# Attention with a low-rank conditioner: x loads and splits placed anew, the projection table shifted by one part

## What is computed

```python
c = x @ W.T + b + 2 * (x @ A[i]) @ B[i]      # A[i], B[i]: rank 16, one pair for each batch
q, k, v = c @ w_q, c @ w_k, c @ w_v           # 32 query heads, 8 key and value heads of 32
x = x + softmax(q k^T / sqrt(32)) v @ w_o
y = x @ weight[j].T                           # one of 8 matrices for each batch
x = x + 4 * sum_e gate_e(y) * (y @ A_e.T) @ B_e.T   # top 2 of 4 experts, rank 16
```

## Time and profile before

| | us |
|---|---|
| median of 3 runs | 1071.86 (1070.69 to 1072.41) |
| the profiled execution | 1075.97 |
| its span | 1074.3 |

### The profile page before, as it was taken

How to read it: one execution, slowest core, us unless ns; L and a number is a source line. 1 busy time by engine, 2 the same in 40 slices (tenths; PEclk the granted TensorE clock), 3 DMA queues, 4 the chain that set the end, 5 groups by cost and what they waited for, 6 DMA issues and landing times.

```text
span 1074.3 us, 17421 instructions
## 1 busy us (share of the span) xinstructions
PE 1018.2 (95%) x6934; PEld 822.1 (77%) x6934; DVE 635.1 (59%) x1071; ACT 450.3 (42%) x782; POOL 233.7 (22%) x224
## 2 busy tenths in 40 slices
PE   7999999999899998999989999899799999999997
PEld 6878787877578775777767787577488898898896
DVE  6562734567755578654776557664555655655653
ACT  5121223355544466543664556544523323323320
POOL 1000001133223333223331236443200100100100
PEclk9999999999899998999998999899989999999998
DMA  7030312011421124211132125435757667667531
GB/s 257 0 99 18 111 55 72 22 36 37 116 57 37 35 53 115 58 34 31 45 97 71 44 81 153 115 115 175 225 165 233 210 189 230 213 184 231 196 118 40
DMA packets 49888, 117.41 MB, mean 109 GB/s; under 512 B 7298, under 2 KB 26114, under 8 KB 45712
## 3 DMA queue, kind: packets, MB, share of 16 engines
q1 hardware_dynamic: 40080, 81.70, 26.0%
q0 software_dynamic: 9728, 34.61, 10.1%
HBM read 86.38 MB, written 18.89 MB: 98 GB/s over the span
## 4 chain that ended last, share of the span: by engine, by line
PE 83%; DVE 6%; ACT 4%; DMA 4%; POOL 1%; SPq 1%; issue 1%; ACTq 0%
PE psP L752 17%; PE psW L1038 16%; PE psF L254 11%; PE psG L1066 8%; PE psO L820 5%; PE psT L807 4%; PE psS L796 4%; PE psP L767 3%; PE psX L1281 3%; PE psO L824 3%; DVE q_stack L652 2%; PE psY L1300 2%; ACT probs L599 2%; ACT q_stack L565 1%; PE psF L265 1%; PE psM L831 1%
## 5 line engine op out<-in xcount | busy, mean ns | idle before, releaser
L672 DVE TENSOR_REDUCE nmax<-psS 128x2 f32<-128x512 f32 x256 | 164.7, 685 | 178.5 <-PE psS L796 176.8
L549 POOL TENSOR_TENSOR p_sum<-probs 128x512 f32<-128x512 f32 x128 | 167.1, 1305 | 395.3 <-ACT probs L599 395.1
L752 PE MATMUL psP<-x_hl,wq 128*128 128x512 f32 x960 | 238.1, 393 | 3.7 <-DVE q_stack L652 3.7
L752 PEld LDWEIGHTS psP<-x_hl,wq 128*128 128x128 f32 x960 | 174.8, 189 | 35.7 <-issue 4.4
L1038 PE MATMUL psW<-wq 128*128 128x256 f32 x1536 | 197.4, 284 | 1.6 <-DVE q_stack L652 1.1
L1038 PEld LDWEIGHTS psW<-wq 128*128 128x128 f32 x1536 | 191.1, 191 | 6.3 <-issue 1.5
L599 ACT ACTIVATE probs<-psT 128x512 f32<-128x512 f32 x256 | 139.1, 595 | 46.9 <-PE psT L807 45.8
L1047 ACT ACTIVATE cond_hi<-cond_raw 128x1024 fp32r<-128x1024 f32 x64 | 66.8, 1057 | 154.3 <-PE psG L1066 149.9
L1051 DVE TENSOR_TENSOR cond_lo<-cond_raw,cond_hi 128x1024 fp32r<-128x1024 f32 x64 | 78.3, 1235 | 89.7 <-ACT cond_hi L1047 89.6
L614 ACT ACTIVATE nmax_rows<-psM 16x128 f32<-16x128 f32 x64 | 17.1, 268 | 190.5 <-PE psM L831 190.5
L652 DVE TENSOR_TENSOR q_stack<-psP,q_stack 32x512 fp32r<-32x512 f32 x128 | 87.8, 686 | 8.0 <-ACT q_stack L565 5.9
(11 more groups left out here) (122 smaller groups left out, 1261.8 us busy)
## 6 DMA issues: line engine op xcount, KB each, us to landing
cond_raw<-in_cond POOLq DMA_DIRECT2D x64, 512.0 KB, 4.0
x_raw<-in_xT SPq DMA_DIRECT2D x32, 256.0 KB, 4.0
q_stack<-q_stack SPq DMA_DIRECT2D x32, 256.0 KB, 3.1
o_scratch<-o_sb SPq DMA_DIRECT2D x64, 128.0 KB
o_raw<-rden_scratch SPq DMA_DIRECT2D x32, 256.0 KB, 5.3
o_raw<-o_scratch SPq DMA_DIRECT2D x8, 1024.0 KB, 9.4
x_sb<-in_xT SPq DMA_DIRECT2D x8, 1024.0 KB, 6.8
outT<-x_sb SPq DMA_DIRECT2D x32, 256.0 KB, 2.5
```

The source lines that it names most:

```text
L549: pool.tensor_tensor(p_sum[:, heads], probs[:, 0, heads], probs[:, 1, heads], ALU.add).then_inc(sum_done, 1)
L672: dve.tensor_reduce(nmax[:, n % 2, 2 * hp:2 * hp + 2, qt], psS[:, i % 2].rearrange("p (h k) -> p h k", h=2), AX.X, ALU.max, negate=True).t ...
L752: mm = pe.matmul(out, wq[:, i, w, k * P:(k + 1) * P], x[:, k, part], start=(k == 0 and n_ == 0), stop=False)
```

## The change

- The table is shifted: q1 of the next pair is finished in s = 15, v0 moves from the second part of s = 0 to the first, q2, v1, v2, v3 and q3 come one part earlier each, the q and k blocks after that are cut otherwise; s = 9 and s = 11 have an empty second part.
- `u` is computed in two halves, one in each part of s = 13; k0 and q0 of the next pair are each whole in a part of s = 14, q1 in two halves in s = 15.
- Six slices of x are loaded at the head of s = 11 on SyncE and two at the head of s = 12, ahead of the rows of maxima. ScalarE splits the six at the end of s = 11, the two in s = 12. VectorE makes the low parts in three places: 0 to 2 in s = 12 after maxima 1, 3 to 5 in s = 12 after the split of maxima, 6 and 7 in s = 13 after maxima 1.
- q7, finished in the first part of s = 12, is evacuated as if it had been finished in the second part: on ScalarE after the exponentials and the x splits, on VectorE in s = 13 after the low parts of slices 6 and 7.
- For the first pair q1 is evacuated ahead of the loop.

```diff
--- before.py
+++ after.py
@@ -278,25 +278,23 @@
 
 
 WORK = [
-    (["q1:4-8"], ["v0"]),
-    (["q2:0-4"], ["q2:4-8"]),
-    (["v1"], ["v2"]),
-    (["v3"], ["q3:0-4"]),
-    (["q3:4-8"], ["k1:0-4"]),
-    (["k1:4-8"], ["q4:0-3"]),
-    (["q4:3-6"], ["q4:6-8"]),
+    (["v0"], ["q2:0-4"]),
+    (["q2:4-8"], ["v1"]),
+    (["v2"], ["v3"]),
+    (["q3:0-3"], ["q3:3-5"]),
+    (["q3:5-8"], ["k1:0-3"]),
+    (["k1:3-6"], ["k1:6-8", "q4:0-2"]),
+    (["q4:2-5"], ["q4:5-8"]),
     (["q5:0-3"], ["q5:3-5"]),
-    (["q5:5-8"], ["q6:0-2"]),
-    (["q6:2-4"], ["q6:4-6"]),
+    (["q5:5-8"], ["q6:0-3"]),
+    (["q6:3-6"], []),
     (["q6:6-8"], ["q7:0-3"]),
-    (["q7:3-5"], ["q7:5-6"]),
+    (["q7:3-6"], []),
     (["q7:6-8"], []),
-    (["+u"], ["+k0:0-5"]),
-    (["+k0:5-8", "+q0:0-2"], ["+q0:2-8"]),
-    (["+q1:0-2"], ["+q1:2-4"]),
+    (["+u:0-4"], ["+u:4-8"]),
+    (["+k0"], ["+q0"]),
+    (["+q1:0-4"], ["+q1:4-8"]),
 ]
-
-FIRST = {0: (["q1"], ["v0"])}
 SEQ = ["u", "k0", "q0", "q1", "v0", "q2", "v1", "v2", "v3", "q3", "k1", "q4", "q5", "q6", "q7"]
 NS = len(SEQ)
 SEQ_DVE = [u for u in SEQ if u[0] != "v"]
@@ -307,7 +305,7 @@
 
 def work(n, part):
 
-    for w in FIRST.get(n, WORK[n % STEPS])[part] if n < N else []:
+    for w in WORK[n % STEPS][part] if n < N else []:
         p = n // STEPS + (w[0] == "+")
         u, _, ks = w.lstrip("+").partition(":")
         first, end = (int(v) for v in ks.split("-")) if ks else (0, KT)
@@ -322,10 +320,12 @@
 
 def evacuated(n, part):
 
-    units = [(p, u) for p, u in finished(n, part) if u != "v0"]
-    if part == 0 and n:
-        units += [(p, u) for p, u in finished(n - 1, 1) if u == "v0"]
-    return units
+
+    behind_x = [(p, u) for p, u in finished(n, 0) if u == "q7" and p + 1 < PAIRS]
+    if part:
+        return finished(n, 1) + behind_x
+    late = [(p, u) for p, u in finished(n - 1, 0) if u == "v0"] if n else []
+    return late + [(p, u) for p, u in finished(n, 0) if u != "v0" and (p, u) not in behind_x]
 
 
 def unit(p, u):
@@ -486,6 +486,9 @@
         def step(n):
             p, s = n // STEPS, n % STEPS
             more = n < N and p + 1 < PAIRS
+            if more:
+                for k in {11: range(0, 6), 12: range(6, KT)}.get(s, ()):
+                    load_x(sp, p + 1, k)
             if 1 <= n <= N:
                 _, _, c, slot = where(n - 1)
                 sp.wait_ge(rows_done, n)
@@ -504,9 +507,6 @@
                 load_den(sp, p - 1)
             if p and n < N and s == 7:
                 store_rden(sp, p - 1)
-            if more:
-                for k in {10: range(0, 3), 11: range(3, 6), 12: range(6, KT)}.get(s, ()):
-                    load_x(sp, p + 1, k)
             for unit_ in evacuated(n, 1):
                 double(*unit_)
             if more and s == 13:
@@ -516,7 +516,7 @@
         sp.wait_ge(before.bp_stored, 32 * CHUNKS)
         sp.wait_ge(before.brow_stored, 16 * CHUNKS)
         load_b(0)
-        for u in ("k0", "q0"):
+        for u in ("k0", "q0", "q1"):
             double(0, u)
         for n in range(N + 3):
             step(n)
@@ -628,7 +628,7 @@
             if more and s == 9:
                 split_a_hi(act, p + 1)
             if more:
-                for k in {11: range(0, 3), 12: range(3, KT)}.get(s, ()):
+                for k in {11: range(0, 6), 12: range(6, KT)}.get(s, ()):
                     split_x_hi(act, p + 1, k)
             for unit_ in evacuated(n, 1):
                 if unit_[1][0] != "v":
@@ -636,7 +636,7 @@
             ahead.scalar(act, n)
 
         act.wait_ge(filled, 3)
-        for u in ("u", "k0", "q0"):
+        for u in ("u", "k0", "q0", "q1"):
             evacuate(0, u)
         for n in range(N + 3):
             step(n)
@@ -686,8 +686,12 @@
             if n < N:
                 maxima(n, 0)
                 maxima(n, 1)
-            for unit_ in evacuated(n - 1, 1) if n else []:
-                evacuate(*unit_)
+            if more:
+                for k in {12: range(0, 3), 13: range(6, KT)}.get(s, ()):
+                    split_x_lo(dve, p + 1, k)
+            for unit_ in evacuated(n - 1, 1) if n else [(0, "q1")]:
+                if unit_[1] != "u":
+                    evacuate(*unit_)
             ahead.vector(dve, n, 0)
             if n < N:
                 maxima(n, 2)
@@ -697,11 +701,14 @@
                 invert(dve, p - 1)
             if more and s == 9:
                 split_a_lo(dve, p + 1)
+            if more and s == 12:
+                for k in range(3, 6):
+                    split_x_lo(dve, p + 1, k)
             for unit_ in evacuated(n, 0):
                 evacuate(*unit_)
-            if more and s == 12:
-                for k in range(KT):
-                    split_x_lo(dve, p + 1, k)
+            for unit_ in evacuated(n, 1):
+                if unit_[1] == "u":
+                    evacuate(*unit_)
             ahead.vector(dve, n, 1)
 
         dve.wait_ge(filled, 3)
@@ -722,11 +729,12 @@
             else:
                 pe.wait_ge(before.tile_lo, CHUNKS * KT)
 
-        def project_u(p):
-            free(p, "u")
-            pe.wait_ge(a_lo_done, p + 1)
+        def project_u(p, first, end):
+            if first == 0:
+                free(p, "u")
+                pe.wait_ge(a_lo_done, p + 1)
             out = psP[0:64, bank(p, "u")]
-            for k in range(KT):
+            for k in range(first, end):
                 pe.wait_ge(x_lo_done, KT * p + k + 1)
                 for c in range(2):
                     cols = slice(c * T, (c + 1) * T)
@@ -735,7 +743,8 @@
                               skip_group_check=True)
                     mm = pe.matmul(out[0:32, cols], a_stack[:, c, k, 0:32], x[:, k, 1, cols], start=False,
                                    stop=(k == KT - 1), skip_group_check=True)
-            mm.then_inc(proj_done, 1)
+            if end == KT:
+                mm.then_inc(proj_done, 1)
 
         def low_rank_ready(p):
             pe.wait_ge(b_landed, 64 * (p + 1))
@@ -770,10 +779,8 @@
 
         def run_work(n, part):
             for p, u, first, end in work(n, part):
-                if n == 0 and u == "q1":
-                    continue
                 if u == "u":
-                    project_u(p)
+                    project_u(p, first, end)
                 elif u[0] == "v":
                     project_v(p, int(u[1]))
                 else:
@@ -850,7 +857,7 @@
                 scores_t(n - 2, 2)
                 scores_t(n - 2, 3)
 
-        project_u(0)
+        project_u(0, 0, KT)
         project(0, "k0", 0, KT)
         project(0, "q0", 0, KT)
         project(0, "q1", 0, KT)
```

## The result

The changed kernel takes 1087.88 us (median of 4, 1087.23 to 1089.3), the kernel before 1072.13 beside it: 1.0137 times as long by the means of the runs, with an interval of 1.0109 to 1.0164. It is slower, to which the forecast gave a chance of 0.51. By the medians it is slower by 15.7 us, where 2.6 were forecast, and outside the range of 1066.5 to 1081.5.

The account below looks back on a forecast made before the run. TensorE, busy 95%, bounds the kernel; only its idle and half-clock time can be won. Passages cost 12.0 us against 11.3, three add 2.1, the last pair 0.5: 1071.86 + 2.6 = 1074.5 us, range 1066.5 to 1081.5.

Parts of the forecast that it names:

- part 7: Steps 1 and 2, per passage: v1 waits 1.4 us for v0's copy, v2 3.9 for q2's slot, half clock 1.5.
- u's wait goes, q2's and the sums' waits go, empty parts cost 0.7: Per passage: u's 5.0 us, q2's 1.2 and steps 9 to 12's 1.8 go; step 9's empty part costs 0.7.
- part 3: Head of step 14: q7's evacuation moves behind VectorE's low splits, TensorE waits 2.2 us per passage, bounds 1.4 and 3.0.
- The half clock at step 14: After step 14's wait of 2.2 us, half clock on TensorE costs 0.6 us per passage.
- parts 1 and 2: Steps 11 and 12: maxima rows queue behind x loads, scores_t waits for exponentials; 1.7 us per passage, 0.9 to 2.4.
- the difference carries over: Whole kernel: profiled execution 1075.97 us, 0.4% over the median 1071.86; the counted 2.6 is added to the median.
- the one on the slower side: Rival: q2's slot wait and v0's late copy bring longer half clock, step 14 pays 1.7; 1080.8 us, chance 0.23.

## Why the prediction was right and wrong

- *The slot and v0's copy* (part 7): right to the tenth. v2 3.71 idle for 3.75, v1 1.23 idle where 1.4 of delay was forecast, in pairs 1 to 3 alone; half clock followed each 3.71 and cost 1.6 to 2.6 for 1.5. Shown by the table's rows put back (20.6 us) and by v0's copy alone (4.4).
- *u's wait goes, q2's and the sums' waits go, empty parts cost 0.7*: right; 0.74 each.
- *The low splits* (part 3), the step that failed: the mechanism was right, VectorE bound, TensorE waiting at the head of step 14; the term was mis-sized. The prediction priced five splits at 3.5 us, from a row of eight in 5.82. In that place TensorE stood idle, and GpSimd had a single sum to make. In the new place, in the middle of two steps, two sums hold them, and 3.5 us became 5.36. TensorE paid 4.3 instead of 2.2 before any clock, 6.3 us over three passages. The sign was in the row itself. Its first split, and a sum of GpSimd that it meets, in the kernel before:

```profile
424.61 1.32 DVE L434 TENSOR_TENSOR x_hl<-x_raw,x_hl 128x512 fp32r<-128x512 f32 x1
424.12 1.27 POOL L549 TENSOR_TENSOR p_sum<-probs 128x512 f32<-128x512 f32 x1 [2.59 <-ACT probs L599]
```

The other seven take 0.68 to 0.69 each, 0.60 from start to start. The average over the eight hid both prices.

- *The half clock at step 14*: 0.6 was taken; two passages of three had 3.4 us of it, about 1.4 each.
- *Loads and high splits* (parts 1 and 2): 1.7 forecast, 2.2 to 2.4 measured; rows did wait behind the loads (0.44 to 0.77). In the terms of the prediction this lies at the upper bound of 2.4; but a cost was looked for in the loads' place, and the run with the loads put back shows that this place is needed.
- *The sum against the median*: "the difference carries over" was a weak step. The first profile of before holds a 6.8 us stretch of half clock in the output stage, about 3.4 us, which its other runs need not have; its second profile lacks it and is 1.2 us shorter. Of the 15.7 us, 11 to 12 arise up to step 12 of the last pair, in both pairs of profiles. Past that point the first pair of profiles has no further loss, and the second has 3.9 us, with half-clock stretches that differ from run to run; why the changed kernel should have more of them on average stays open.
- *The direction*: the sum had the loss at 2.6 us and the chance of slower at 0.51; that it is slower by this much was not foreseen.
- *The rivals*: the one on the slower side came nearest, 1080.8, with half clock as its mechanism; the larger part was the held splits, which no rival named.

## What to carry to other kernels

When an instruction is moved, price it by a row from a place with the same neighbours: a row from a stretch in which the other engines nearly stood still is a lower bound. When a projection is pulled forward by one part, follow its evacuation to the last reader of the buffer that it overwrites, since everything queued behind that copy, and the next user of its PSUM bank, pays. Spread waits seem cheaper than one wait of the same length: half clock followed a wait of 3.71 us in six of six passages and one of 2.48 in four of six (two profiles of the changed kernel), and waits of 0.2 to 0.9 in one of six (q7 early, with and without the table's rows). That one shows that short waits are no guarantee.

## What the runs showed of the hardware

A VectorE operation that reads two SBUF tensors (the low split) and starts while GpSimd's two-input addition is running waits for its end: 1.78 us instead of 0.68, and at most 0.69 in all 32 cases once GpSimd's additions beside it are two columns wide. The cast of eight maxima behaves alike (mostly 0.66 to 0.87 us, 0.17 without) and ends 0.03 us after the addition. The traces show the like the other way, without a run of its own: an addition that starts with a split or early in it lasts 1.70 to 1.84 us instead of 1.28. Operations that read PSUM (q7's lows, 2.78 for four, and maxima, 1.29 for two) are not touched by it. The Trainium skill says in "GPSIMD Engine Reference", section "8. Key points", that GpSimd shares its SBUF interfaces with VectorE and contends with its instructions in a two-port mode or with two SBUF inputs. The splits, which have two SBUF inputs, agree, and show that it is the whole rest of the GpSimd instruction that is waited for.
